# A layer-norm statistics change in a cross-attention and FP4 feed-forward layer: two row tiles in one bn_stats

## The reference

```
def layernorm(x, gamma, beta):
    mu = jnp.mean(x, axis=-1, keepdims=True)
    var = jnp.var(x, axis=-1, keepdims=True)
    return (x - mu) * jax.lax.rsqrt(var + EPS) * gamma + beta

# x is (8, 512, 256), ctx is (8, 64, 256), EPS is 1e-5
y  = norm(x)                                             # no gain or shift
y  = layernorm(y + attention(y, y, y, causal=True), g1, beta1)
y  = layernorm(y + attention(y, ctx, ctx, causal=False), g2, beta2)
y  = layernorm(y + relu(y @ w1 + b1) @ w2 + b2, g3, beta3)
x  = x + y
h  = norm(x)                                             # no gain or shift
g, u = fp4_linear(h, w_gate), fp4_linear(h, w_up)        # 704 wide
x  = x + fp4_linear(silu(g) * u, w_down)
```

## Time and profile before

| | |
|---|---|
| median of 3 runs | 655.77 us (655.36 to 656.45) |
| the profiled execution, its own time | 655.71 us |
| its span, first to last instruction | 653.9 us |
| TensorE matmul, busy | 574.1 us, 88%, 3989 instructions |
| VectorE, busy | 525.4 us, 80%, 1300 instructions |
| ScalarE, busy | 382.2 us, 58%, 781 instructions |
| GpSimd, busy | 355.8 us, 54%, 450 instructions |
| chain that ended last | TensorE 53%, VectorE 25%, issue 9%, ScalarE 6%, GpSimd 3% |

### The profile page before, as it was taken

One profiled execution on the slowest core, in us unless ns is written; L12 is line 12 of the kernel. 1 busy time (PEld: TensorE's weight loads), 2 busy tenths in 40 slices (PEclk: granted clock), 3 DMA queues, 4 the chain that ended last, 5 costly groups with the idle time before them and its releaser, 6 DMA issues.

```text
span 653.9 us, 12396 instructions
## 1 busy us (share of the span) xinstructions
PE 574.1 (88%) x3989; PEld 540.5 (83%) x3989; DVE 525.4 (80%) x1300; ACT 382.2 (58%) x781; POOL 355.8 (54%) x450
## 2 busy tenths in 40 slices
PE   3776769998999999999999899999999898988665
PEld 2665759898989898998989898989899898978565
DVE  3788677898878888888879888888889878988663
ACT  3456365665738575666657574766666664746331
POOL 3555363575646555575557555655657554654521
PEclk9777889999999999999999999999999999999886
DMA  7600000010100101010101010010101010000000
GB/s 223 207 2 33 1 15 28 1 49 1 41 18 20 32 1 58 0 48 0 56 0 48 1 32 24 0 48 0 56 2 33 2 33 2 18 1 18 0 17 16
DMA packets 18742, 19.30 MB, mean 30 GB/s; under 512 B 1536, under 2 KB 18192, under 8 KB 18704
## 3 DMA queue, kind: packets, MB, share of 16 engines
q1 hardware_dynamic: 18704, 18.82, 9.3%
HBM read 14.62 MB, written 4.19 MB: 29 GB/s over the span
## 4 chain that ended last, share of the span: by engine, by line
PE 53%; DVE 25%; issue 9%; ACT 6%; POOL 3%; DMA 1%; SPq 1%; DVEq 0%; POOLq 0%; ACTq 0%
PE R L925 4%; PE R L927 4%; PE R L926 4%; PE O L973 4%; PE O L1040 3%; PE O L1038 3%; PE O L1039 3%; PE TR L811 3%; PE R L992 3%; DVE hs L1314 3%; PE R L994 3%; PE R L993 3%; PE R L811 3%; DVE hT_lo L1341 3%; DVE hqT_lo L1347 2%
## 5 line engine op out<-in xcount | busy, mean ns | idle before, releaser
L456 POOL TENSOR_TENSOR rs<-mv,neg_half 128x1 f32<-128x1 f32 (+1 forms) x112 | 69.6, 627 | 47.3 <-DVE mv L1261 45.7
L925 PE MATMUL R<-gu_hi,xqT_hi 128*128 128x352 f32 x256 | 87.2, 341 | 4.3 <-issue 3.3
L992 PE MATMUL R<-y2T_hi,w_hi 128*128 128x256 f32 x256 | 76.6, 299 | 9.2 <-DVE y2T_lo L1397 6.5
L926 PE MATMUL R<-gu_lo,xqT_hi 128*128 128x352 f32 x256 | 83.9, 328 | 0.0
L927 PE MATMUL R<-gu_hi,xqT_lo 128*128 128x352 f32 x256 | 83.8, 327 | 0.0
L462 POOL TENSOR_TENSOR hs<-hh,h_rec 128x704 f32<-128x704 f32 x32 | 44.6, 1393 | 69.2 <-DVE h_rec L1297 69.2
L677 ACT ACTIVATE hqT_hi<-R 128x768 fp32r<-128x768 f32 x32 | 26.0, 813 | 90.7 <-PE R L811 90.7
L1038 PE MATMUL O<-w_hi,hT_hi 128*128 128x256 f32 x256 | 73.7, 288 | 0.0
L994 PE MATMUL R<-y2T_hi,w_lo 128*128 128x256 f32 x256 | 72.7, 284 | 0.0
L993 PE MATMUL R<-y2T_lo,w_hi 128*128 128x256 f32 x256 | 72.6, 284 | 0.0
L1039 PE MATMUL O<-w_lo,hT_hi 128*128 128x256 f32 x256 | 72.4, 283 | 0.0
(11 more groups left out here) (153 smaller groups left out, 1827.7 us busy)
## 6 DMA issues: line engine op xcount, KB each, us to landing
x_in<-in_x SPq DMA_DIRECT2D x16, 256.0 KB, 2.8
x_res<-in_x SPq DMA_DIRECT2D x16, 256.0 KB, 2.9
out<-x SPq DMA_DIRECT2D x32, 128.0 KB, 1.7
ctx_rows<-in_ctx SPq DMA_DIRECT2D x16, 64.0 KB, 2.5
hT<-in_L_xattn_w SPq DMA_DIRECT2D x1, 1024.0 KB, 7.9
hh<-in_L_xattn_w SPq DMA_DIRECT2D x1, 768.0 KB, 8.4
wd_raw<-in_L_ffn_w_down SPq DMA_DIRECT2D x1, 704.0 KB, 9.5
w_raw<-in_L_ffn_w_gate SPq DMA_DIRECT2D x1, 640.0 KB, 4.6
```

Of the source, the lines that this page charges most:

```text
L456: pool.tensor_tensor(rs[i][:, t0:t0 + len(ts)], mv[i][:, t0:t0 + len(ts), 1], neg_half[:, 0:len(ts)], ALU.pow).then_inc(ln_rstd[i], 1)
L925: mm(o, xh, gu_hi[:, c, m, cols], start=(c == 0), stop=False)
L926: mm(o, xh, gu_lo[:, c, m, cols], start=False, stop=False)
L992: mm(o, w1_hi[:, c, cols], y2T_hi[:, c, :], start=(c == 0), stop=False)
```

## The change

Where two tiles are ready together, one bn_stats reads both, and in such an order that element k of one tile is followed by element k of the other. Its even elements are then the one tile and its odd elements the other, and the six numbers are already count, mean and sum of squared deviations of each. No aggregation follows; one tensor_scalar (`variance`) makes (sum of squares) / 256 + EPS for both tiles, and shifts and norms read the mean where bn_stats wrote it. This is done for x_in, z1 and z2 (`pair_stats`). For the first time x1 of tile 0 and z3 of tile 1 also go together (`both_stats`, number 5, BOTH), read through a view of the buffer in which both lie, with one power for the two. z3 of tile 0 and x1 of tile 1 keep bn_stats, aggregation and their own power.

```diff
+        z3_x1 = [w_raw[:, T * 1 + 1:T * (3 + i) + 1:T * (2 + i) - 1, :] for i in range(2)]
...
+        ALONE, BOTH = (3, 4), 5
+        st = [sb(f"st{i}", [P, 9] if i in ALONE else [P, T, 3]) for i in range(6)]
+        mv = [sb(f"mv{i}", [P, 2]) for i in range(6)]
...
             # GpSimd
-                    power(4, b, g, F, (0,))
-                    power(3, b, g, F, (1,))
+                    power(BOTH, b, g, F)
...
             # VectorE
+            def pair_stats(i, src):
+                v.bn_stats(st[i][:].rearrange("p t s -> p (t s)"),
+                           src.rearrange("p t d -> p d t")).then_inc(ln_stat[i], 1)
+
+            def variance(i, b, h, lag):
+                wait_alone(dve, ln_stat[i], b, h, lag, 1, 1)
+                v.tensor_scalar(mv[i][:], st[i][:, :, 2], 1.0 / D, EPS, ALU.mult, ALU.add).then_inc(ln_aggr[i], 1)
+
+            def shift(i, b, h, lag):
+                wait(dve, ln_rstd[i], b, h, lag, 1, 1)
+                v.scalar_tensor_tensor(nm[i][:], st[i][:, :, 1], -1.0, rs[i][:],
+                                       ALU.mult, ALU.mult).then_inc(ln_shift[i], 1)
...
+            def both_stats(b, h):
+                wait(dve, x1_set, b, h, F, T, 1)
+                wait(dve, z3_set, b, h, F, T, T)
+                pair_stats(BOTH, z3_x1[(h - F) % 2])
...
                 if f1:
                     x1_sum(b, g, 0)
-                    x1_stats(b, g, 0)
-                    aggregate(4, b, g, F, 0)
-                    z3_stats(b, g, 1)
-                    aggregate(3, b, g, F, 1)
+                    both_stats(b, g)
+                    variance(BOTH, b, g, F)
                     x_norm(b, g, 0)
                     x_max(b, g, 0)
                     x_scale(b, g, 0)
                     x_reciprocal(b, g, 0)
-                    shift(3, b, g, F, (1,))
+                    z3_shift(b, g, 1)
...
-                    stats(1, b, h, A, 0, z1)
-                    stats(1, b, h, A, 1, z1)
-                    aggregate(1, b, h, A, 0)
-                    aggregate(1, b, h, A, 1)
+                    pair_stats(1, z1[:])
+                    variance(1, b, h, A)
...
                 if front:
-                    aggregate(0, b, h + 1, 0, 0)
-                    aggregate(0, b, h + 1, 0, 1)
+                    variance(0, b, h + 1, 0)
...
-                    stats(2, b, h, A, 0, z2)
-                    stats(2, b, h, A, 1, z2)
-                    aggregate(2, b, h, A, 0)
-                    aggregate(2, b, h, A, 1)
+                    pair_stats(2, z2)
+                    variance(2, b, h, A)
```

More of the change, by code:

```diff
@@ L164, in layer_program @@
                   (xa[:], T * IC // 2, FC))
[L166 to L169, removed]
+        ALONE, BOTH = (3, 4), 5
+        st = [sb(f"st{i}", [P, 9] if i in ALONE else [P, T, 3]) for i in range(6)]
+        mv = [sb(f"mv{i}", [P, 2]) for i in range(6)]
+        rs = [sb(f"rs{i}", [P, 1 if i in ALONE else T]) for i in range(6)]
+        nm = [sb(f"nm{i}", [P, T]) for i in range(4)]
         R = es.enter_context(nc.psum_tensor("R", [P, 4 * 512], F32))
@@ L449, in prepare, with power @@
                         pool.wait_ge(shift2_set, 1)
[L451 to L457, removed]
+            def power(i, b, h, lag):
+                n = 1 if i in ALONE else T
+                wait(pool, ln_aggr[i], b, h, lag, 1, 1)
+                pool.tensor_tensor(rs[i][:], mv[i][:, 1:2] if i in ALONE else mv[i][:],
+                                   neg_half[:, 0:n], ALU.pow).then_inc(ln_rstd[i], 1)
             def scale_h(b, h, t):
@@ L521, in slot @@
                     unscale_x(b, g, 0)
-                    power(4, b, g, F, (1,))
+                    power(4, b, g, F)
                 if f:
@@ L530, in slot @@
                 if a:
-                    power(1, b, h, A, (0, 1))
+                    power(1, b, h, A)
                 if live(b, h, 0):
@@ L551, in slot @@
                 if live(b, h + 1, 0):
[L552 removed]
+                    power(0, b, h + 1, 0)
                 prepare(b, h, "gain")
@@ L629, in prepare, with norm @@
                             act.activation(w2_hi[:, f0:f1, :], raw, ACT.Copy).then_inc(w2_hi_set, 1)
[L631 to L634, removed]
+            def norm(i, b, h, lag, t, src, dst):
+                r, c = (BOTH, 0) if i == 3 and t == 1 else (i, t)
+                n = T if i == 3 else 1
+                wait(act, ln_rstd[r], b, h, lag, 1, 1)
+                wait(act, ln_shift[i], b, h, lag, n, t + 1 if i == 3 else 1)
                 act.activation(dst, src, ACT.Identity, bias=nm[i][:, t:t + 1],
-                               scale=rs[i][:, t:t + 1]).then_inc(ln_out[i], 1)
+                               scale=rs[r][:, c:c + 1]).then_inc(ln_out[i], 1)
             def xT_upper(b, h, t):
@@ L1215, in w_lower @@
                 v.tensor_tensor(dst, src, f32(hi), ALU.subtract).then_inc(wq_lo, 1)
[L1217 to L1220, removed]
+            for i in ALONE:
+                v.memset(st[i][:, 6:8], 0.0).then_inc(ln_eps, 1)
+                v.memset(st[i][:, 8:9], EPS * D).then_inc(ln_eps, 1)
+            dve.wait_ge(ln_eps, 4)
             for m in range(2):
@@ L1434, in x_stats @@
                 wait(dve, ln_out[0], b, h, 1, T, T)
-                for t in range(T):
-                    stats(0, b, h, 0, t, x_in[par])
+                pair_stats(0, x_in[par][:])
             def slot(b, h):
@@ L1446, in slot @@
                 if f1:
-                    shift(3, b, g, F, (0,))
+                    z3_shift(b, g, 0)
                 if a:
@@ L1509, in slot @@
                 if a:
-                    shift(1, b, h, A, (0, 1))
+                    shift(1, b, h, A)
                 if f:
```

82 lines of the change are left out of this document (42 added, 40 removed).

## The result

The changed kernel took 661.63 us (median of 4 runs, 660.00 to 663.66) where the kernel before took 655.57 beside it (4 runs, 651.23 to 656.45). The ratio is 1.0095, 95% interval 1.007 to 1.012. It is slower, by about 6 us; the forecast was 660.4, from 4.8 us of loss.

What follows compares the result with a forecast made beforehand. TensorE (88% busy) was held by VectorE's ordered work before the attention scores and before the transpose of ce. Terms +4.2 - 0.6 + 1.2 = +4.8 us on 655.7 gave 660.5, taken as 660.4; range 655.6 to 672.

Steps and rivals of the forecast that it cites:

- The joint statistics of x1 and z3: Before x_norm: power no longer overlapped, x_norm 0.38 us late, TensorE's scores 0.38 (h = 1) or 0.20 (h = 0); 4.2 together.
- The cost of hopping: Pair bn_stats alternating between tiles: no loss likeliest; rival up to 0.52 us more per pair, centre 672 us, chance 0.15.
- The variance in the gap: x_in's variance between down_add and second h_product waits for GpSimd's multiplication: 0.11 us late in eleven slots, +1.2 us.
- z2: z2's variance waits for GpSimd's scale_h of the second tile; 0.55 us idle before ff_sum pays for it, cost 0.
- z1 and x_in: Paired statistics in mid-slot: 0.1 us gained in six slots with h = 0, nothing with h = 1; -0.6 us.
- The sum: Whole kernel: +4.2 - 0.6 + 1.2 = +4.8 us on the profiled execution's 655.7 us.
- Slot 3: First slot with the x1 block, where x1's power is on the chain of waits: another 0.4 us lost.

Runs made afterwards that it cites:

- e1: Changed kernel with x1 and z3 given separate bn_stats, aggregations and one-column powers again, pairs for x_in, z1 and z2 kept; 655.49 us.
- e2: Changed kernel with only x1 and z3 joint; x_in, z1 and z2 back to a bn_stats and an aggregation per tile; 658.40 us.
- e4: Changed kernel with the two-column power for x1 and z3 cut into two one-column powers, x1's first; 658.69 us.
- e5: Changed kernel with each pair's bn_stats reading one tile after the other instead of alternating elements, so the statistics are not computed rightly; 661.3 us.
- e3: Changed kernel with the variance of x_in moved between h_max and h_scale of tile 0, where GpSimd is idle; 658.81 us.
- e6: Changed kernel with x1 and z3 separate, x_in's variance between h_max and h_scale, z2's variance behind z3's bn_stats; 653.69 us, ratio 0.9976.
- e8: Kernel before, statistics unchanged, with h = 1 hT_lower of tile 1 directly behind x_norm and the z3 shift; 654.16 us.

## Why the prediction was right, step by step

**The joint statistics of x1 and z3.** Predicted: x_norm 0.38 late, TensorE 0.38 and 0.20 late, idle about 0.8. Measured: x_norm 0.42 late, TensorE 0.39 and 0.22, idle 0.82. e1 and e2 show that this part causes it over the steady slots, e4 that the second column of the power is 0.15 of it. The three terms of the step (0.26 for the second tile, 0.17 for the variance, 0.70 for the power) were measured at 0.28, 0.17 and 0.70. The lesson of it is cover: two statistics in a row hid the first power, and one for both hides nothing. The full period of e2 is 0.41 and 0.23 longer than before, so nothing behind the scores took the delay back.

**The cost of hopping.** Predicted as the likeliest case: none. Measured in e5: 0.02 us of 0.71. By the Trainium skill's figure for a hopping source (Vector Engine (DVE) Microarchitecture Reference, section Measured stream behaviour on trn2) it would have been 0.35 a pair, as an estimate; the runs do not bear it out for bn_stats. What the same section says of a read stream that alternates between two regions and writes one word for two read, that it ran at the full rate, fits.

**The variance in the gap.** Predicted: it ends with GpSimd's multiplication, 0.11 late. Measured: it ends 0.02 after it, and the wait before ce is 0.09 longer in e1 in both kinds of slot. On VectorE itself the stretch from the start of h_max to that of cross_max is 0.14 longer with h = 0 (5.42 against 5.28) and 0.07 with h = 1, so this term was a little too small. The same tensor_scalar took 0.35 under the multiplication and 0.16 outside it (e3). That agrees with the Trainium skill, page SBUF — State Buffer, section Who interferes with whom, by which a tensor_scalar can take the port pair shared with GpSimd; the rows add that an instruction of two columns is held up as a long one is.

**z2.** Predicted: the variance stands until scale_h ends, the 0.55 idle before ff_sum pays for it. GpSimd, then VectorE of the changed kernel, answering to the earlier trace rows:

```profile
403.80 1.39 POOL L464 TENSOR_TENSOR hs<-hh,h_rec 128x704 f32<-128x704 f32 x1 [2.06 <-DVE h_rec L1316]
```

```profile
403.64 0.64 DVE L1267 BATCH_NORM_STATS2 st<-w_raw 128x6 f32<-128x512 f32 x1
404.42 0.79 DVE L1273 TENSOR_SCALAR mv<-st 128x2 f32<-128x2 f32 x1
405.13 0.42 DVE L1259 BATCH_NORM_STATS2 st<-w_raw 128x6 f32<-128x256 f32 x1
...
405.88 0.42 DVE L1383 TENSOR_TENSOR w_raw<-O,b_row 128x256 f32<-128x256 f32 x1
```

The variance ends at 405.21, 0.02 after scale_h, and ff_sum starts without any idle. The cover was used up to the last hundredth, and e6, which takes the stall away, is no shorter by it.

**z1 and x_in.** This is the step that was mis-sized. Predicted: 0.10 gained with h = 0. In e1, where this is nearly all that is left of the change beside the gap, a slot with h = 0 is 0.13 longer and its wait before ce 0.09 longer, just as with h = 1 (0.11 and 0.09): no more than about 0.02 of the gain arrives at TensorE. VectorE itself gains 0.06 there with h = 0: from z1's bn_stats to h_max it takes 4.06 us in the changed kernel and 4.12 before. The second pair starts 1.08 after the first (352.61 to 353.69), where 1.01 was predicted and it had been 1.10. With h = 1 the copy behind the shift of z1 is longer. VectorE of the kernel before, then VectorE and GpSimd of the changed kernel:

```profile
386.56 0.17 DVE L1267 SCALAR_TENSOR_TENSOR nm<-mv,rs 128x2 f32<-128x2 f32 x1
386.65 0.68 DVE L1341 TENSOR_TENSOR hT_lo<-hT,hT_hi 128x512 fp32r<-128x512 f32 x1
```

```profile
391.38 0.15 DVE L1278 SCALAR_TENSOR_TENSOR nm<-st,rs 128x2 f32<-128x2 f32 x1
391.45 1.27 DVE L1360 TENSOR_TENSOR hT_lo<-hT,hT_hi 128x512 fp32r<-128x512 f32 x1
```

```profile
391.43 0.74 POOL L500 TENSOR_TENSOR w_raw<-x_res,beta_row 128x256 f32<-128x256 f32 x1
```

The copy takes 1.27 instead of 0.68, while GpSimd's second residual sum beside it takes 0.74 instead of 1.25. The longer copy uses up the 0.47 idle of the earlier trace rows, so from z1's bn_stats to h_max it is 4.59 against 4.58 and costs nothing. At the same place of a slot with h = 0 the copy takes 0.68 as before. The prediction had put a limit on the gain (GpSimd's sum) but not drawn it down far enough.

**The sum.** For a steady pair of slots the prediction has 0.38 + 0.20 + 0.22 - 0.10 = 0.70. Measured is 0.92 (35.86 + 36.36 against 35.44 + 35.86), of which e2 has 0.64 and e1 0.24. All of the difference is in the slots with h = 0. With h = 1 it predicts 0.49 and 0.50 came; with h = 0 it predicts 0.21 and 0.42 came. The listed waits of TensorE there grew by 0.22 and 0.10. The remaining 0.1 lies between the scores and ce, where the rows show it in two places without a listed wait: the first gate_up product is followed by the next after 0.26 us instead of 0.22, and the transpose of xq by its successor after 0.19 instead of 0.14. What holds them is not shown.

The total was also helped by luck. Added up over the stretches of the table above, the prediction's terms are 0 to slot 2, 4.1 over the twelve slots, 0.6 in slots 15 to 17 and 0.15 in the tail. Measured were 0.9, 5.3, 1.9 and -2.2. So the direction, the place and the largest term were right. But up to slot 17 it came to 8.1 us where 4.7 were predicted, in part at a lower clock, and a shorter tail, which nothing in the prediction has, gave 2.2 of it back. Slot 3, for which the prediction has 0.4, cannot be judged: its period differs by 1.6 between the changed kernel and e5.

What stays open: what holds TensorE for the last 0.1; whether the clock of the tail goes with the kernel; and with it why the medians of e1 and e2 do not add up to that of the whole change. The period of slot 16, 35.2 in the changed kernel and in e3 but 34.0 to 34.3 in all others, falls together with the granted clock: 0.79 and 0.87 in two neighbouring stretches of 5 us in the changed kernel (from 560 and 565 us) and 0.83 over 10 us in e3, where the kernel before has 1.00 throughout.

## What to carry to other kernels

Merging operations that are "ready together" joins their latencies: where one operation's short wait (here a power on another engine) was hidden behind the other's work, the merged form exposes it, so count the path to the first consumer and not the instructions saved. Merge where both results are used late, keep apart where the first is waited for (e6 against the change), and look whether the new form of an operation is held up by another engine where the old one was not (here 0.35 us instead of 0.16). When a stand-still on the bounding engine is found, first ask what else stands in the releaser's order before it: moving the awaited piece forward gained 2.1 us over twelve slots (e8), where the pairs, well placed, gained 1.3 (e6).

## What the runs showed of the hardware that I had not expected

- A bn_stats that changes between two tiles at each element runs at nearly the rate of a straight one: 711 against 694 ns and 709 against 688 for 512 values. So means and variances of two tiles come from one instruction, the even half being one tile, for 0.71 us where two separate ones in a row took 0.75.
- A tensor_scalar of two columns, 0.17 us long, took 0.35 and 0.79 when it met a GpSimd multiplication, and ended 0.02 us after it. A bn_stats of two tiles beside the same multiplication kept its 0.64 (z2 above).
- A GpSimd power of one column takes 0.55 us and one of two columns 0.70, so a second column inside one instruction costs 0.15 and outside it 0.5 (e4 has 1.06 for two in a row).
